# A gated cross-attention block: queries, latent keys and latent values made once for all batches, and two context tiles turned at once

## The reference

```python
xn = layer_norm(ctx, gamma_x, beta_x)              # 8 x 375 x 256
ln = layer_norm(_layernorm(x), gamma_l, beta_l)    # 8 x 112 x 256
q = (ln @ Wq) * d ** -0.5                          # 512 columns: 8 heads of 64
k_x, v_x = split(xn @ Wkv); k_x = rope_rotate_k(k_x)
k_l, v_l = split(ln @ Wkv)
k = concatenate([k_x, k_l], 2); v = concatenate([v_x, v_l], 2)   # 487 rows
attn = softmax(einsum('bhid,bhjd->bhij', q, k))
x = x + tanh(g_xattn) * (einsum('bhij,bhjd->bhid', attn, v) @ Wo)
x = x + tanh(g_ffn) * moe(_layernorm(x))           # softmax router, top 2 of 8, gelu MLP 256-1024-256
```

## Time and profile before

| | |
|---|---|
| device time, median of 3 runs | 526.6 us (524.97 to 527.88) |
| the profiled execution | 523.4 us, with a span of 521.7 us |
| PE busy | 446.3 us, 86% of the span |
| ACT, DVE, POOL busy | 295.1, 289.4 and 195.4 us |
| mean granted clock of TensorE | 0.928 |

### The profile page before, as it was taken

How to read it: one execution, slowest core, us unless ns; L and a number is a source line. 1 busy time by engine, 2 the same in 40 slices (tenths; PEclk the granted TensorE clock), 3 DMA queues, 4 the chain that set the end, 5 groups by cost and what they waited for, 6 DMA issues and landing times. The chain is left out here.

```text
span 521.7 us, 9510 instructions
## 1 busy us (share of the span) xinstructions
PE 446.3 (86%) x3237; PEld 373.2 (72%) x3237; DVE 289.4 (55%) x707; ACT 295.1 (57%) x652; POOL 195.4 (37%) x223
## 2 busy tenths in 40 slices
PE   2674699999989999899998764589999999999990
PEld 1453476766767677676776643279999999999990
DVE  3784324244451634435254823558888888888850
ACT  3534466765666666766767411056667667776730
POOL 4530163462825538164460165302222222333222
PEclk9976699999999999999999875569999999999997
DMA  7400010000000008999000021785777778775323
GB/s 190 117 29 1 1 31 0 9 24 2 29 1 24 5 0 252 226 215 319 12 2 1 1 71 44 233 254 175 212 204 212 219 223 232 224 206 132 44 29 90
DMA packets 41864, 56.04 MB, mean 107 GB/s; under 512 B 1745, under 2 KB 37153, under 8 KB 41808
## 3 DMA queue, kind: packets, MB, share of 16 engines
q1 hardware_dynamic: 36864, 49.80, 32.2%
q0 software_dynamic: 4960, 5.72, 7.1%
HBM read 40.37 MB, written 16.07 MB: 108 GB/s over the span
## 5 line engine op out<-in xcount | busy, mean ns | idle before, releaser
L1367 POOL DMA_INDIRECT acc_scratch<-yv,xt x28 | 49.2, 1757 | 130.6 <-DVE yv L1520 126.3
L1389 ACT ACTIVATE hf<-ph,b1t 128x256 f32<-128x256 f32 x112 | 47.0, 471 | 48.4 <-PE ph L1595 47.8
L871 DVE TENSOR_REDUCE negmax<-sc 112x1 f32<-112x487 f32 x64 | 42.2, 660 | 46.4 <-PE sc L1103 46.4
L691 ACT ACTIVATE prob<-sc,negmax 112x487 f32<-112x487 f32 x64 | 43.5, 680 | 12.6 <-DVE negmax L871 9.4
L1128 PEld LDWEIGHTS po<-probt,vals 125*64 125x64 f32 (+1 forms) x512 | 25.4, 139 | 23.5 <-issue 15.6
L699 ACT COPY probt<-pt 125x448 f32<-125x448 f32 x64 | 34.7, 542 | 11.1 <-PE pt L1111 10.9
L1103 PE MATMUL sc<-keys,queries 64*112 64x488 f32 x128 | 35.3, 629 | 6.1 <-ACT keys L640 3.4
L1502 DVE TENSOR_TENSOR hl<-hf,hh 128x512 fp32r<-128x512 f32 x56 | 38.8, 693 | 1.9
L1111 PEld LDWEIGHTS pt<-ident,prob 112*125 112x125 f32 x256 | 36.6, 191 | 4.2
L1111 PE MATMUL pt<-ident,prob 112*125 112x112 f32 x256 | 38.3, 274 | 0.0
L1500 DVE CAST hh<-hf 128x512 fp32r<-128x512 f32 x56 | 24.2, 433 | 23.7 <-ACT hf L1389 23.2
(11 more groups left out here) (273 smaller groups left out, 1372.1 us busy)
## 6 DMA issues: line engine op xcount, KB each, us to landing
w_next<-in_L_ffn_W SPq DMA_DIRECT2D x10, 1024.0 KB
rows_scratch<-blank SPq DMA_DIRECT2D x2, 4257.0 KB, 33.4
w_third<-in_L_ffn_W SPq DMA_DIRECT2D x8, 1024.0 KB
w1s<-in_L_ffn_W SPq DMA_DIRECT2D x5, 1024.0 KB
w2s<-in_L_ffn_W SPq DMA_DIRECT2D x5, 1024.0 KB, 8.7
xt<-rows_scratch SPq DMA_DIRECT2D x14, 258.0 KB, 2.8
ctx_t<-in_ctx SPq DMA_DIRECT2D x8, 375.0 KB
w1s<-in_L_xattn_Wkv SPq DMA_DIRECT2D x1, 1024.0 KB, 12.3
```

The costliest lines, as they stand in the source:

```text
L691: act.activation(prob[:, h % 2, 0:JA], sc[h % 2][0:M, 0:JA], ACT.Exp, bias=negmax[:, h % 2:h % 2 + 1], accum_out=total[:, p, h:h + 1]).the ...
L871: dve.tensor_reduce(negmax[:, h % 2:h % 2 + 1], sc[h % 2][0:M, 0:JA], AX, ALU.max, negate=True).then_inc(max_done.sem, 1)
L1367: pool.indirect_dma_start(out=acc_dram, out_offset=bass.IndirectOffsetOnAxis(ap=xt[i % 3][:, n, D + 1:D + 2].bitcast(I32), axis=0), in_=yv ...
L1389: last = act.activation(hf[:, n % 3, u], ph[n % 3][:, u * T:(u + 1) * T], ACT.Gelu, bias=b1t[:, col])
```

## The change

The change takes everything that depends on the latents out of the batches.

- **Latents.** They are loaded and treated in two halves of four batches. The two layer norms are made one (the second is worked out from the variance of the first). A half is turned with eight transposes and split by one operation per 128 rows.
- **Queries and latent keys** of a half are made already turned: 128 columns of the weights are the stationary operand, and the 448 tokens of the half stream, one group per pair of heads. That gives eight groups for the queries and eight for the keys, kept in `qall` (by ACT) and `kall` (by DVE; it lies in the buffer of the second expert's weights).
- **Latent values** are eight products, one for each batch, kept in `vall` by DVE (in the buffer of the first expert's weights).
- **Copies.** In step 14 DVE copies the queries, latent keys and latent values of one batch to `queries`, `keys` and `vals` (`copy_latents`). The steps of before for these three are gone.
- **Context.** Tiles 0 and 1 are turned and split together, then tile 2. LEAD is 8. Statistics stand at s 0, the normalisation at 2, the other steps later as in the tables below.
- **Beginning.** The steps of batch 0 are interleaved with `latents(s)`, and batch 1 starts at AHEAD = 13, before the first scores. The low part of Wq is made by POOL. SP loads both halves of the latents and Wkv before the context, and loads experts' weights only after the last `copy_latents`.

The core of the diff:

```diff
-        LEAD = 6
+        LEAD = 8
+        AHEAD = 13
-        def frame(eng, prepare, other_latents, begin, head, close):
-            for s in range(H + 1):
-                prepare(0, 0, 2 * s, first=True)
-                prepare(0, 0, 2 * s + 1, first=True)
-                other_latents(s)
+        def frame(eng, prepare, latents, begin, head, close):
+            for s in range(AHEAD + LEAD - 2):
+                prepare(0, 0, s, first=True)
+                latents(s)
+                if s >= AHEAD:
+                    prepare(0, 1, s - AHEAD)
             begin(0, 0)
-            for s in range(LEAD):
+            for s in range(LEAD - 2, LEAD):
                 prepare(0, 1, s)
...
+            load_latents(1)
+            sp.dma_start(w1s[:, :, :], wkv...).then_inc(wkv_loaded, 16)
             load_context(0, 0)
-            for done in (wkl_done, wvals_done, wql_done):
-                sp.wait_ge(done, 1)
+            sp.wait_ge(lat_done.sem, lat_done.at(B // 2 - 1, 1, 3))
...
 ACT
+            high_latents(0)
+            high_weights(slice(0, INNER))
+            keep_queries(0, 0)
+            keep_queries(0, 1)
+            high_weights(slice(INNER, 2 * INNER))
+            high_latents(1)
+            for n in range(2, 2 * HP):
+                keep_queries(n // HP, n % HP)
             def prepare(t, p, s, first=False):
+                if s == 4:
+                    split_context(t, p, 0)
+                if s == 7:
+                    split_context(t, p, 1)
+                if s == 8:
+                    raw_key(t, p, 0)
+                if s == 9:
+                    keep_value(t, p, 0)
+                if s == 10:
+                    raw_key(t, p, 1)
+                if s == 11:
+                    keep_value(t, p, 1)
+                if s == 12:
+                    raw_key(t, p, 2)
+                if s == 13:
+                    keep_key(t, p, 0)
+                    keep_value(t, p, 2)
+                if s == 16:
+                    keep_key(t, p, 1)
+                if s == 18:
+                    keep_key(t, p, 2)
...
 DVE
+            def copy_latents(t, p):
+                b = bass.ds(2 * t + p, 1)
+                cols = bass.ds((2 * t + p) * M, M)
+                dve.wait_ge(score_done.sem, score_done.at(t, p, -H))
+                dve.wait_ge(qall_done, 2 * HP)
+                dve.tensor_copy(queries[:, p], qall[:, :, cols]).then_inc(lat_done.sem, 1)
+                dve.wait_ge(kall_done, 2 * HP)
+                dve.tensor_copy(keys[:, p, :, J:JA], kall[:, :, cols]).then_inc(lat_done.sem, 1)
+                dve.wait_ge(av_done.sem, av_done.at(t, p, -HP))
+                dve.wait_ge(vall_done, B)
+                dve.tensor_copy(vals[0:M, p, JT], vall[:, b]...).then_inc(lat_done.sem, 1)
+            latent_stats(0)
+            latent_norm(0)
+            latent_stats(1)
+            ...
+            split_latents(0)
+            latent_norm(1)
+            split_latents(1)
...
 PE
+            turn_latents(0)
+            latent_queries(0, 0)
+            latent_queries(0, 1)
+            turn_latents(1)
+            for n in range(2, 2 * HP):
+                latent_queries(n // HP, n % HP)
+            def latents(s):
+                if s in (3, 4):
+                    for a in range(HP):
+                        latent_keys(s - 3, a)
+                if 6 <= s < 6 + B:
+                    latent_values(s - 6)
             def prepare(t, p, s, first=False):
+                if s == 3:
+                    transpose_context(t, p, 0)
+                if s == 6:
+                    transpose_context(t, p, 1)
+                if s == 7:
+                    project_keys(t, p, 0)
+                if s == 8:
+                    project_values(t, p, 0)
+                if s == 9:
+                    project_keys(t, p, 1)
+                if s == 10:
+                    project_values(t, p, 1)
+                if s == 11:
+                    project_keys(t, p, 2)
+                if s == 12:
+                    transpose_keys(t, p, 0)
+                    project_values(t, p, 2)
+                if s == 15:
+                    transpose_keys(t, p, 1)
+                if s == 17:
+                    transpose_keys(t, p, 2)
```

More of the change, by code:

```diff
@@ L255, in attention @@
         out_t, heads = sb("out_t", [P, HP, M]), sb("heads", [P, HP, M])
-        lf = [keys[:, 1, n, 0:KD * M].rearrange("p (k m) -> p k m", k=KD) for n in range(2)]
+        lf = [w[:].rearrange("p a m -> p (a m)") for w in (out_t, heads)]
         tp, pk, pv, po = ps("tp"), ps("pk"), ps("pv"), ps("po")
@@ L756, in close @@
                 keep_turned(B - 1)
-            frame(act, prepare, other_latents, begin, head, close)
+            frame(act, prepare, latents, begin, head, close)
         @block.vector
@@ L795, in affine_latents @@
                 for k in range(KD):
[L796 to L816 removed]
+                    dve.wait_ge(lhigh_done, KD * g + k + 1)
@@ new lines, in split_latents @@
+                    if g:
+                        dve.wait_ge(llow_done, k + 1)
+                    dve.tensor_scalar(lf[k], (sc, pt)[g][k][:, 0:HALF], affine[:, 2, k:k + 1],
+                                      affine[:, 3, k:k + 1], ALU.mult, ALU.add).then_inc(lfull_done, 1)
+                for k in range(KD):
+                    dve.wait_ge(lfull_done, KD * g + k + 1)
+                    dve.tensor_tensor(tokl[:, k, columns(g)], lf[k], tokh[:, k, columns(g)].bitcast(F32),
+                                      ALU.subtract).then_inc(llow_done, 1)
@@ new lines, in latent_queries @@
+            def latent_queries(g, a):
+                n = g * HP + a
+                if n == 0:
+                    pe.wait_ge(wql_done, 1)
+                pe.wait_ge(llow_done, KD * (g + 1))
+                if n >= 4:
+                    pe.wait_ge(qall_done, n - 3)
+                c = slice(a * P, (a + 1) * P)
+                product(GROUP_BANKS[n % 4][:, 0:HALF],
+                        [(wqh[:, k, c], wql[:, k, c], tokh[:, k, columns(g)], tokl[:, k, columns(g)])
+                         for k in range(KD)]).then_inc(qgroup_done, 1)
@@ new lines, in latent_keys @@
+            def latent_keys(g, a):
+                n = g * HP + a
+                if n == 0:
+                    pe.wait_ge(wkl_done, 1)
+                if n >= 4:
+                    pe.wait_ge(kall_done, n - 3)
+                else:
+                    pe.wait_ge(qall_done, HP + n + 1)
+                c = slice(a * P, (a + 1) * P)
+                product(GROUP_BANKS[n % 4][:, 0:HALF],
+                        [(wkvh[:, k, c], wkvl[:, k, c], tokh[:, k, columns(g)], tokl[:, k, columns(g)])
+                         for k in range(KD)]).then_inc(kgroup_done, 1)
@@ L1023, in project_values @@
-            def project_values(t, p, n):
-                rows, ah, al = rows_of(t, p, n)
-                if n == 0:
-                    pe.wait_ge(queries_done.sem, queries_done.at(t, p, 1))
-                    pe.wait_ge(wvals_done, 1)
-                else:
-                    pe.wait_ge(vals_done.sem, vals_done.at(t, p, n))
-                product(pv[0:rows, :], [(ah[:, k], al[:, k], wkvh[:, k, INNER:], wkvl[:, k, INNER:])
-                                        for k in range(KD)]).then_inc(vproj_done.sem, 1)
@@ new lines, in _, with transpose_context @@
+            latent_queries(0, 1)
+            turn_latents(1)
+            for n in range(2, 2 * HP):
+                latent_queries(n // HP, n % HP)
+            def transpose_context(t, p, n):
+                pe.wait_ge(cnorm_done.sem, cnorm_done.at(t, p, PART[n].stop))
+                if n == 0:
+                    pe.wait_ge(keys_done.sem, keys_done.at(t, p, -1))
+                else:
+                    pe.wait_ge(cf_done.sem, cf_done.at(t, p, 1))
+                for i, j in enumerate(range(PART[n].start, PART[n].stop)):
+                    for k in range(KD):
+                        last = pe.transpose(tp[:, (i * KD + k) * JR:(i * KD + k + 1) * JR],
+                                            ctx_t[:, p, j, k * P:(k + 1) * P], ident[0:JR, 0:JR])
+                last.then_inc(ctr_done.sem, 1)
@@ new lines, in project_keys @@
+            def project_keys(t, p, j):
+                pe.wait_ge(cl_done.sem, cl_done.at(t, p, 1 if j < 2 else 2))
+                if j == 0:
+                    pe.wait_ge(keys_done.sem, keys_done.at(t, p, 0))
+                else:
+                    pe.wait_ge(kraw_done.sem, kraw_done.at(t, p, j))
+                product(pk[0:JR, :], [(ch[:, j, k], cl[:, j, k], wkvh[:, k, 0:INNER], wkvl[:, k, 0:INNER])
+                                      for k in range(KD)]).then_inc(kproj_done.sem, 1)
```

453 lines of the change are left out of this document (175 added, 278 removed).

## The result

The changed kernel takes 532.5 us (median of 4 runs, 532.0 to 533.3), the kernel before 526.3 beside it (4 runs, 525.0 to 527.9). Ratio 1.0133, 95% interval 1.0106 to 1.0159: slower by 1.3%. The profiled execution has a span of 530.3 us, against 521.7.

A forecast was written before the change was run, and what follows sets the result against it. PE was taken to bound the batches and latency the beginning. 523.4 - 7.7 (batches) + 11.6 (beginning) = 527.3 for the profiled execution, 530 against the median; own range 524 to 536, with rivals 516 to 542.

The forecast's parts named there:

- The beginning: Time until batch 0's head 0 scores after its first pair: 77 us against 65.4, +11.6, ends +4.6 and +16.
- The first four query groups: PE's first groups in the beginning: start at 17 to 18, 1.24 us each, first at half clock, done by 25.8.
- the items after the last product: DVE's rotation, value copy, batch 1 statistics, copies and normalisation, with POOL's power, after 63; PE turns batch 1's tiles at 69.2.
- The batches: All batches together: 30.2 us each instead of 31.65 in 1 to 5; in sum -7.7 us, ends -13 and 0.
- The four stretches: A batch cut where heads 0, 2, 4, 6 issue scores (S0, S2, S4, S6): 10.6, 8.2, 6.2, 5.2 us.
- rival B: PE's clock falls in each batch after idling before head 4's scores: 2 us more in each of 7, 544; chance 0.11.
- PE's clock at 1.00 through the batches: Sign expected in the profile: PE's granted clock stays at full, 1.00, in the batches.
- S2 to S4: From head 2's scores to head 4's: chain through values copy, exponential and three DVE copies; 8.2 us against 6.38.
- Rival C: The three latent copies wait for POOL's rotation, up to 1.3 us more for each of two; 537; chance 0.06.
- Rival A: Batches gain more than the beginning loses: 27.8 us a batch, beginning at +8, 517 to 520; chance 0.22.
- S4 to S6: From head 4's scores to head 6's: context statistics and normalisation ahead of maxima; 6.2 us against 6.76.
- S6 to S0: From head 6's scores to the next head 0's: two context splits ahead of the exponentials; 5.2 us against 7.45.

The follow-up runs named there:

- copies early: Changed kernel with DVE's three latent copies in head 1 of the batch before instead of head 3; 528.1 us, 1.0046 of the kernel before.
- all: Changed kernel with key, value and latent copies, output and context statistics, normalisation, batch 1's preparation and POOL's subtractions all moved; 517.0 us, 0.9844 of the kernel before.
- stats early: Changed kernel with DVE's context statistics and normalisation, and POOL's power, in heads 0 and 1 instead of 4 and 5; 528.2 us, 1.0041 of the kernel before.
- output late: Kernel "all" with the context's normalisation and the previous batch's output statistics moved to head 3; 498.1 us, 0.9467 of the kernel before.

## Why the prediction was right, and where not

**The time.** 530 was forecast, 532.5 measured; a loss of 3.4 us against 6.2. Its own sum, 527.3, stands against 532.0 for the profiled execution. The mechanism was right in both parts; the gain of the batches was put at twice what came.

**The beginning** was forecast at +11.6 and measured at +12.15. The steps held: the half of the latents landed at 9.9 (forecast 11, 9.5 to 13), the first group started at 16.5 (17 to 18), the context of batch 1 was turned at 69.13 (69.2) after 5.24 us of idle time (5), the first scores came at 72.75 (71.8). Two delays that I had not named, the subtraction of 2.00 and the normalisation of 3.11, ate what the earlier landing gave. Two sums of this part don't follow from their terms. The first four query groups, started at 17 to 18 and of 1.24 each with the first at half clock, end at 23.2 to 24.2 and not at 25.8; they ended at 24.7, since two took 2.3 each, and the wait behind them, to 26.0, hid it. And the items after the last product, one behind the other from 63 on, end at 70.7 and not at 69.2. It came out at 69.1 because the rotation began at 62.73, before the last product ended, and POOL's power ran beside the copies; the text doesn't say so, and so this term was right in part by luck.

**The batches** were forecast at -7.7 and measured at -3.7. The four stretches were right to 0.3 us where the clock was full: 10.47, 8.22, 6.1 and 5.4, against 10.6, 8.2, 6.2 and 5.2. The term that was mis-sized is the clock, which the text put into rival B as 2 us in every batch or none; its sign "PE's clock at 1.00 through the batches" failed, it was 0.94. It was low after S4 in four of seven: 7.44, 7.61 and 7.62 instead of 6.1 in batches 0, 1 and 4, and 6.22 in batch 2, where it fell too late to cost more than 0.1; 4.5 us in all. Without them the batches come to -8.2. A batch took 30.8 on average, within the 28.5 to 32 that the text allowed. Why it fell ahead of S4 in one batch, behind it in another and in batches 3, 5 and 6 not at all stays open. Batches 2 and 4 have the same order and the same 2.5 us of PE idle in S2 to S4; windows of 2 us, two of batch 2 and one of batch 4:

```profile
157.00:159.00 2.00, 2.00 (x24) 1.29 (x20) 1.90 (x11) 0.41 (x1) 0.23 (x1) 0.78 0.00 0
159.00:161.00 2.00, 2.00 (x12) 1.65 (x8) 1.34 (x6) 1.49 (x4) 0.63 (x1) 0.50 0.00 0
```

```profile
216.00:218.00 2.00, 0.87 (x2) 0.45 (x4) 1.35 (x6) 1.66 (x4) 0.00 (x0) 0.54 1.02 208
```

**The chain in S2 to S4.** That the exponential of head 4 starts right behind the copy of the values, at 4.75, was right (4.68), and so was the cost of the copies on the chain (0.95 to 1.0; "copies early"). The picture that the values copy was the only thing ahead was not: DVE's statistics of the output end 0.6 us before the reciprocal, so taking the one away gave 0.7 and not the 1.6 I then expected. I had them in the earlier trace rows and used the row only for the lock, not for the place of the statistics in DVE's queue.

**Rival C** (the copies wait for POOL) was rightly given little: at 154.12 they took 0.39, 0.39 and 0.42, the last rotation having ended at 152.56. Moved into head 1, one of them did wait, 1.50 ("copies early"). The rule of the Trainium skill, "SBUF — State Buffer", section "Who interferes with whom", fits these runs: it names copies and tensor_scalar in a two-port mode and operations with two SBUF inputs as those that exclude GpSimd, and the normalisation, a tensor_scalar, took 4.36 instead of 1.06 beside the rotations, while bn_stats took 1.07 both with POOL idle and beside it.

**Rival A** (faster) did not come true for the order as it was changed, but its argument, 5 us less of PE's work in a batch, was sound: with the waits moved a batch takes 26.7 to 26.8 and the whole 5.3% less than before. How much of that the same moves would bring to the kernel before was not tried. Its price was wrong: 2.4 us less in each of five batches and 3.6 in the beginning take the forecast of 530 to 514, not to 517 to 520. So was that of rival C: two waits of 1.3 on 30.2 make 32.8 a batch, not 31.7.

## What to carry to other kernels

When work leaves the engine that bounds, lay out the chain that takes over link by link, and for every link list all that is queued ahead of it on its engine, not only the latest: the next wait can be 0.6 us behind the first. Then move what doesn't need to be on the chain into the stretches where the bounding engine is busy anyway, but keep DVE operations between SBUF places out of the time of GpSimd's passes wherever something on the chain stands behind them. A change that frees the bounding engine and loses is not yet judged: here the same operations in another order took 34 us less.

## What the runs showed of the hardware

- **DVE and GpSimd hold each other for whole operations.** A normalisation of three tiles took 1.06 us by itself, 3.11 beside one GpSimd operation of 2.37 and 4.36 beside a row of them; a subtraction of one element in each of 112 partitions 0.15 or 1.26. GpSimd waits as well: a pass of 1.27 took 1.94 beside DVE's copies ("copies early"). Statistics of three tiles (bn_stats) took 1.07 with GpSimd idle and beside it ("all"). Sums over an execution hide it: DVE's busy time rose by 26 us with the same 715 instructions ("stats early").
- **PE's clock after short waits.** With PE idle for 2.3 to 2.7 us in S2 to S4 the granted clock went to half in four batches of seven, from 1.0 us ahead of S4 to 1.6 behind it ("changed"). With 1.3 to 1.4 there and 1.8 in S4 to S6 it fell at the start of S6 to S0, in five of seven ("copies early"). With 0.6, 0.7 to 0.8 and 0.4 to 0.5 it never fell ("output late", batches 0 to 5). The idle time alone doesn't say whether it falls: batches 2, 3 and 4 of "changed" had the same 2.5 us, and it fell in two of them. A fall cost 1.3 to 1.6 us where it came at the start of a stretch, 2.4 once ("stats early", batch 0), so the two kernels without any gained more than the sum of their stretches at full clock.
